# Projecting the next pair's q and k early in the odd steps, and laying both out in the same step

## The reference, cut to what matters

```python
mod = (_silu(c) @ wmod).reshape(16, 6, 1, -1)          # sa, ca, ga, sb, cb, gb
h = _layernorm(x) * (1 + ca) + sa
qkv = h @ W_qkv + b_qkv                                # 16 heads of 8 features
energy = jnp.einsum('bqhe,bkhe->bqhk', q, k)
attn = jax.nn.softmax(energy, axis=-1) / sqrt(E)
out = jnp.einsum('bihv,bvhd->bihd', attn, v).reshape(B, N, E) @ W_out + b_out
x = x + ga * out
h = _layernorm(x) * (1 + cb) + sb
x = x + gb * (quantise_fp6(h) @ quantise_fp6(weight).T + bias)   # blocks of 32
```

## Time and profile before

| | |
|---|---|
| median of 3 runs | 371.02 us (368.11 to 371.32) |
| profiled execution, its own time | 370.78 us |
| span of the profiled execution | 368.9 us |
| mean granted TensorE clock | 0.837 of full speed |
| PE busy | 304.0 us (82%) |
| VectorE, ScalarE, GpSimd busy | 245.1 (66%), 211.6 (57%), 174.5 us (47%) |
| DMA, mean busy share of 16 engines | 42.9% for the queue of SyncE |

### The profile page before, as it was taken

One profiled execution on the slowest core, in us unless ns is written; L12 is line 12 of the kernel. 1 busy time (PEld: TensorE's weight loads), 2 busy tenths in 40 slices (PEclk: granted clock), 3 DMA queues, 4 the chain that ended last, 5 costly groups with the idle time before them and its releaser, 6 DMA issues.

```text
span 368.9 us, 7149 instructions
## 1 busy us (share of the span) xinstructions
PE 304.0 (82%) x2506; PEld 175.0 (47%) x2506; DVE 245.1 (66%) x581; ACT 211.6 (57%) x404; POOL 174.5 (47%) x330
## 2 busy tenths in 40 slices
PE   1741997899969996999599987999699969999952
PEld 1211873455536453646255544546364636565521
DVE  5586895467957794579548784579557866984334
ACT  5470044478648862677357853677467745777720
POOL 5900133038563855265624765275535643547431
PEclk9966556599989995799759995799779996999985
DMA  5597079105930593128710692039602881010000
GB/s 151 170 306 156 26 245 227 50 1 228 202 92 32 230 206 73 44 114 237 157 30 16 240 225 57 30 124 253 131 30 96 248 177 33 18 46 4 17 14 14
DMA packets 23970, 43.81 MB, mean 119 GB/s; under 512 B 2144, under 2 KB 7408, under 8 KB 23936
## 3 DMA queue, kind: packets, MB, share of 16 engines
q1 hardware_dynamic: 23936, 43.37, 42.9%
HBM read 23.93 MB, written 18.91 MB: 116 GB/s over the span
## 4 chain that ended last, share of the span: by engine, by line
PE 37%; DMA 33%; POOL 12%; DVE 10%; issue 4%; SPq 2%; ACT 1%; POOLq 0%; DVEq 0%; ACTq 0%
DMA k_rows<-parts_dram 23%; PE ps_p L793 14%; DMA parts_dram<-qk_parts 10%; PE ps_o L823 9%; DVE neg_max L683 3%; POOL qk_parts L319 2%; POOL xh L296 2%; PE ps_pre L850 2%; POOL rstd L448 2%; PE ps_pre L834 2%; POOL xm L300 2%; POOL h L304 2%; PE ps_pre L844 2%; PE ps_post L881 2%; PE ps_o L867 1%
## 5 line engine op out<-in xcount | busy, mean ns | idle before, releaser
L683 DVE TENSOR_REDUCE neg_max<-ps_p 128x2 f32<-128x512 f32 x256 | 167.1, 684 | 84.7 <-PE ps_p L793 83.3
L552 ACT ACTIVATE probs<-ps_p 128x512 f32<-128x512 f32 x256 | 146.2, 594 | 93.1 <-PE ps_p L808 90.9
L793 PE MATMUL ps_p<-k_rows,q_rows 62*128 62x256 f32 x512 | 132.8, 364 | 35.3 <-DMA k_rows<-parts_dram 35.3
L793 PEld LDWEIGHTS ps_p<-k_rows,q_rows 62*128 62x128 f32 x512 | 87.2, 221 | 100.8 <-issue 48.2
L808 PE MATMUL ps_p<-q_rows,k_rows 64*128 64x256 f32 x512 | 130.1, 354 | 1.8 <-ACT probs L552 1.8
L823 PE MATMUL ps_o<-probs,v_aug 128*32 128x256 f32 x1024 | 90.5, 442 | 0.2 <-ACT probs L552 0.2
L808 PEld LDWEIGHTS ps_p<-q_rows,k_rows 64*128 64x128 f32 x512 | 84.0, 211 | 7.3 <-ACT probs L552 5.6
L429 POOL CAST max_parts<-neg_max 128x16 fp32r<-128x16 f32 x32 | 6.3, 197 | 88.8 <-DVE neg_max L683 88.8
L823 PEld LDWEIGHTS ps_o<-probs,v_aug 128*32 128x32 f32 x1024 | 23.5, 116 | 22.0 <-issue 7.6
L448 POOL TENSOR_TENSOR rstd<-ve,minus_half 128x2 f32<-128x2 f32 x16 | 11.3, 704 | 37.7 <-DVE ve L608 37.7
L319 POOL TENSOR_TENSOR qk_parts<-qk_full_sb,qk_parts 128x512 fp32r<-128x512 f32 x14 | 17.9, 1275 | 11.5 <-ACT qk_parts L533 11.5
(11 more groups left out here) (104 smaller groups left out, 362.0 us busy)
## 6 DMA issues: line engine op xcount, KB each, us to landing
parts_dram<-qk_parts SPq DMA_DIRECT2D x8, 1024.0 KB, 4.5
parts_dram<-qk_parts SPq DMA_DIRECT2D x16, 512.0 KB, 3.7
q_rows<-parts_dram SPq DMA_DIRECT2D x16, 512.0 KB, 6.9
k_rows<-parts_dram SPq DMA_DIRECT2D x16, 512.0 KB, 9.3
modb<-mod_rows_dram SPq DMA_DIRECT2D x16, 256.0 KB, 3.3
out_dram<-out_sb SPq DMA_DIRECT2D x16, 128.0 KB, 1.7
x_all<-in_L_attn_x_dram SPq DMA_DIRECT2D x1, 1536.0 KB, 9.3
q_rows<-maxT SPq DMA_DIRECT2D x64, 8.0 KB
```

Source lines behind the costliest of these rows:

```text
L552: act.activation(probs[:, v % 2, u % 4, :], ps_p2[:, u % 2, :], ACT.Exp).then_inc(exp_done, 1)
L683: dve.tensor_reduce(neg_max[:, half, :, r, j], ps_p1[:, (16 * b + s) % P1_BANKS, :].rearrange("p (q k) -> p q k", q=QT), AX_X, ALU.max, ne ...
L793: ins = pe.matmul(ps_p1[:, (16 * b + s) % P1_BANKS, t * T:(t + 1) * T], q_rows[64 * r:64 * r + ROWS1, slot, i, e, t * P:(t + 1) * P], k_ro ...
```

## The change

q is projected in slot 2 and k in slot 4 of the odd step, v of batch b+1 in slot 7 of every step. ACT saves hT in slot 1 behind the exponential, hdT in slot 2, q in slot 3, k in slot 5 ahead of onT, v in slot 7. GpSimd makes both low parts right behind `split_max(b+1, 0)`, ahead of `attn_weights(b)`. SyncE stores both parts ahead of `place_max(b+1, 0)` and issues the four layout loads in the same odd step, between `place_max(b+1, 0)` and `place_max(b+1, 1)`. Waits on `ps_pre` follow the new order: k waits for q's save, v for k's, half 0 of the maxima for v's.

```diff
@@ SyncE
             for b in range(-1, NB + 2):
-                early, late = low_pair(b), low_pair(b - 1)
+                p = low_pair(b)
...
-                if late is not None:
-                    lay_out(late, 0)
-                    lay_out(late, 1)
                 if has(b + 1) and b >= 0:
                     load_modb(b + 1)
                 if has(b - 2):
                     store(b - 2)
+                if p is not None:
+                    store_parts(p, 0)
+                    store_parts(p, 1)
                 if has(b + 1):
                     place_max(b + 1, 0)
-                if early is not None:
-                    store_parts(early, 0)
-                    store_parts(early, 1)
+                if p is not None:
+                    for kind in range(2):
+                        for r in range(2):
+                            lay_out(sp, p, kind, r)
                 if has(b + 1):
                     place_max(b + 1, 1)
@@ GpSimd
                     split_max(b + 1, 0)
+                if low_pair(b) is not None:
+                    low_part(pool, low_pair(b), 0, q_saved)
+                    low_part(pool, low_pair(b), 1, k_saved)
                 if has(b):
                     attn_weights(b)
                 if norm_pair(b) is not None:
                     normalise1(norm_pair(b), 0)
-                if low_pair(b) is not None:
-                    low_part(pool, low_pair(b), 0, q_saved)
...
-                if low_pair(b) is not None:
-                    low_part(pool, low_pair(b), 1, k_saved)
@@ ScalarE
-                    if s == 0 and pre is not None:
+                    if s == 1 and pre is not None:
                         save_hT(pre)
...
-                    if s == 1 and has(b - 2):
+                    if s == 2 and has(b - 2):
                         save(b - 2, hdT_full, f_full, hdT[:, :], ps_post[:, 0:T], hdT_saved)
-                    if s == 4 and has(b + 1):
-                        save_v(b + 1)
+                    if s == 3 and pre is not None:
+                        save_qk(pre, 0, q_full, q_saved)
+                    if s == 5 and pre is not None:
+                        save_qk(pre, 1, k_full, k_saved, ps_post if pre < 2 else ps_pre)
                     if s == 5 and has(b - 1):
                         save(b - 1, onT_full, y_full, onT[:, :], ps_post[:, 0:T], onT_saved)
-                    if s == 5 and pre is not None:
-                        save_qk(pre, 0, q_full, q_saved)
+                    if s == 7 and has(b + 1):
+                        save_v(b + 1)
...
-                    if s == 10 and pre is not None:
-                        save_qk(pre, 1, k_full, k_saved, ps_post if pre < 2 else ps_pre)
@@ TensorE
+                    if s == 2 and pre is not None:
+                        project_qk(pre, 0, q_full, ps_pre)
...
-                    if s == 4 and has(b + 1):
-                        project_v(b + 1)
+                    if s == 4 and pre is not None:
+                        if pre < 2:
+                            project_qk(pre, 1, k_full, ps_post, (modT_ready, 1), (k_saved, 2 * pre))
+                        else:
+                            project_qk(pre, 1, k_full, ps_pre, (q_saved, 2 * (pre + 1)))
...
-                    if s == 5 and pre is not None:
-                        project_qk(pre, 0, q_full, ps_pre, (v_saved, b + 2))
...
+                    if s == 7 and has(b + 1):
+                        project_v(b + 1, (k_saved, 2 * (pre + 1) if pre is not None else 0))
                     if s == 8 and has(b + 1):
-                        transpose_max(b + 1, 0, (q_saved, 2 * (pre + 1) if pre is not None else 0), (v_saved, b + 2))
-                    if s == 10 and pre is not None:
...
+                        transpose_max(b + 1, 0, (v_saved, b + 2))
```

More of the change, by code:

```diff
@@ L320, in low_part, with lay_out @@
                               qk_parts[:, p % 2, kind, 0, :].bitcast(F32), ALU.subtract).then_inc(low_ready, 1)
+        def lay_out(eng, p, kind, r):
+            wait(eng, (parts_stored[kind], 16 * (1 + kind) * (p + 1)), (p2_full, 16 * 2 * (p - RING + 1)))
+            if p < RING:
+                eng.wait_ge(rows_filled[p], 2)
+            rows = q_rows if kind == 0 else k_rows
+            by_row = parts_dram[p, kind].rearrange("(i r d) q t -> r (d q) i t", r=2, d=D)
+            dst = rows[64 * r:64 * r + QUAD, p % RING, :, :, :].rearrange("a i e t -> a i (e t)")
+            eng.dma_start(dst.bitcast(F32), by_row[r]).then_inc(laid_out[p % RING], 16)
         block = ctx.enter_context(nc.Block())
@@ L354, in store_parts @@
                                      ).then_inc(parts_stored[1], 16)
[L356 to L365, removed]
             def place_max(b, half):
@@ L388, in _ @@
             store_parts(0, 1)
-            lay_out(0, 0)
-            lay_out(0, 1)
+            for kind in range(2):
+                for r in range(2):
+                    lay_out(sp, 0, kind, r)
             sp.wait_ge(rows_ready, 1)
@@ L835, in transpose_x, with project_v @@
                 ins.then_inc(xT_full, 1)
-            def project_v(b):
-                wait(pe, (hT_saved, 2 * (b // 2 + 1)), (maxT_saved, 2 * b))
+            def project_v(b, *before):
+                wait(pe, (hT_saved, 2 * (b // 2 + 1)), (maxT_saved, 2 * b), *before)
                 if b == 0:
@@ L955, in _ @@
                     if s == 14 and has(b + 1):
-                        transpose_max(b + 1, 1, (k_saved, 2 * (pre + 1) if pre is not None else 0),
-                                      (maxT_saved, 2 * b + 3))
+                        transpose_max(b + 1, 1, (maxT_saved, 2 * b + 3))
                     if s in (13, 15) and has(b):
```

## The result

The changed kernel takes **345.06 us** in the median of 4 runs (344.02 to 345.97), against 371.13 us for the kernel before (4 runs): ratio 0.931, 95% interval 0.926 to 0.937. The profiled execution took 344.02 us, its span is 342.2 us.

What follows compares the result with a forecast made beforehand. PE's waits for k's layout, paid as idle time and slow clock, were taken as the bound. Six pairs save 23.8 us, pair 1 adds 0.5, one slow pair 3: 20.3 off 370.78 gives 350.5 us, range 338 to 369.

Steps and rivals of the forecast that it cites:

- case A: Whole kernel: the sum of the terms holds, 350.5 us, range 344 to 357; chance 0.42.
- The timing inside the odd step: Odd step, from slot 0: k's low part done at 11.2 us, first load issued at 14.9, k's layout landed at 28.1.
- the step on what is late next: Slot 8': half 1 of the maxima, queued behind the loads, lands near 28.7 us; PE waits 0.7 us.
- Rival C: Slots 8' and 12': half 1 isn't held back, no waits, a pair takes 34.6 us, kernel 340 us; chance 0.15.
- The pair: Each of six pairs: 34.6 us plus a wait of 0.7 us makes 35.3, for 39.3 before.
- moving v costs nothing new: Projecting v in slot 7, not slot 4: same four matmuls, v needed only in the next step, no added cost.
- The sixth pair: Last of the six pairs, counted at 35.3 us like the others; the six together 211.8 us.
- The clock: Six pairs: waits of 0.8, 1.2 and 0.7 us leave it at 1.00, save one slow pair costing 3 us.
- Rival B: Slot 8': the wait is some 2 us, half clock follows, a pair takes 38.0 us, kernel 364 us; chance 0.25.
- Pair 1: First steps: slot 8 waits for the copy at 61.5 us, slot 12 at 65.5 to 66.5; counted as +0.5 us.
- Rival D: Slots 1 to 5: ACT saves pile up at half clock, 41.5 us a pair, kernel 385 us; chance 0.13.
- E: Whole kernel: nothing changes, as the copy of half 1 takes back exactly what the layout gives; chance 0.05.

Runs made afterwards that it cites:

- the loads alone: Kernel before with only the four layout loads moved to the odd step, behind the stores and ahead of half 1 of the maxima: 377.1 us, ratio 1.026.
- the copy in ACT's queue: Changed kernel with half 1 of the maxima issued by ScalarE's own queue in odd steps, behind its save in slot 14: 356.0 us, ratio 0.956.
- the kernel with half loads: Kernel before with half of the layout loads' data left out for pairs 1 to 7, as many transfers: 335.5 us, ratio 0.898.
- all three edits: Changed kernel with onT saved ahead of k, split_max(b+1, 1) before modulate2's last product, v and hdT in old slots where no pair is projected: 342.2 us, ratio 0.926.

## Why the prediction was right

The forecast was 350.5 us, rounded to 351, and 345 came, by the mechanism of case A, with some luck in the pair and the clock. By its steps:

- **The timing inside the odd step.** k's low part ends 11.5 us after slot 0 (forecast 11.2), the first load is issued at 15.6 (14.9), k's layout lands at 28.0 (28.1), the second scores of slot 8' start at 28.5 (half 1 at 28.7). The rows of before, laid end to end in the new order, gave these within 0.7 us.
- **The wait that follows.** It moved from slot 12' to slot 8', behind the loads in the queue, as the step on what is late next has it. Shown by the loads alone (39.3 us of waits for half 1 where 26.5 for the layout were) and by the copy in ACT's queue (no wait). Its size is 0 to 0.5 us a pair, 0.2 in the mean, against 0.7. Rival C is out. The Trainium skill (DMA: Bandwidth & Descriptors, "Queues, rings and completion order") has both sides, ring order within a queue and completion that need not follow it; here the copies were held up behind the loads of their queue, 7 times of 7 in the kernel with the loads alone.
- **The pair.** 35.2 us against 35.3, but that it came so near is luck: three waits were smaller than forecast, by 1.2 us in all, and two terms were missing, of 0.5 and some 0.8 us. onT's wait is 0.78 (forecast 1.2), q's 0.50 (0.8). Not in the sum was the wait of PE in slot 14 for `max_parts`, 0.5 to 0.7 us, twice a pair: the row for it stood in the late steps of before (0.68 us in one), and I took 15.0 us for a late step without asking what was in it, so the even half had it and the odd half not. And "moving v costs nothing new" was wrong by 0.4 us a step, together with hdT's save; the late steps show it. The slow clock of a pair before was worked out from a pair of 32.6 us, and the kernel with half loads has 33.3 at full clock.
- **The sixth pair** was mis-sized. I took 35.3 for all six, but the stretch from step 11 to step 13 takes 33.0 us (transposes of oT at 249.74 and 282.70). Its first half takes 17.5 us as in the others; its second takes 15.5, as a late step, for it ends in step 13, which has no transposes of x and no q of a next pair. The six take 209.0, not 211.8: 2.8 of the 6.5 us that were missing.
- **The clock.** "I take the clock to stay at 1.00, save for one pair" held without the exception: the pair after pair 1 took 35.2 at 1.00, another 3 us, for the half clock behind slot 8 of pair 1 was over by 67 us. The reason given was too bold, though. The rows had only waits of some 3.8 us, and I set waits of 0.7 to 1.2 against them as safe. The other kernels show the half clock behind waits of 0.89, 1.08, 1.13 and 1.31 us. The forecast 1.2 us for onT lies among these; that 0.78 came, and that the clock held, is in part luck. Rival B was nearer than its chance of 0.25 says: a like thing happens with loads 5 us later, at the wait of slot 12' in place of 8'. Its 364 us is no check of its sum, which has a wait of 1.1 us in it (the copy at 29.1, slot 8' at 28.0) where its condition says some 2; with 2 us it gives 38.9 us a pair and 369. The Trainium skill (TensorE: Matmul & The Clock Gate, "HAM oscillation — how this bites in real kernels") tells of a kernel whose clock was throttled behind each wait for a transfer. The runs agree for the waits of 1.08, 1.54, 1.63, 1.97 and 2.50 us named above, and disagree for those of 0.84 us and less, and for 1.30 and 1.76.
- **Pair 1.** Slot 8 waited until 61.87 (forecast 61.5); the transposes of oT in step 1 came at 73.7, 1.9 us sooner than before, where I had +0.5. Of that the tail gave back 1.8 (59.5 us from the last such transposes to the end, 57.7 before), whose steps are 0.4 longer each.

Rival D's build-up of saves on ACT is there only as the short waits for q's save and onT, and E's balance isn't.

Where did the 26.8 us between the profiled executions come from? 26.5 us of waits for the layout went; 2.6 us came for the maxima, and the short waits for onT, q's save, `max_parts` and hdT (5.1, 3.4, 7.7 and 1.8 us) grew from 2.4 to 18.0 us. The view of the earlier trace rows has for the kernel before, with none for q's save:

```profile
PE ps_pre L857 <- POOL max_parts L431: 1.4, 2, 0.7
...
PE ps_post L895 <- ACT hdT L556: 0.5, 1, 0.5
PE ps_post L881 <- ACT onT L556: 0.5, 1, 0.5
```

By the waits some 18 us are left over, and PE's busy time, 19.5 us shorter for the same matmuls, says where they are: in the slots at half clock that are gone (forecast 2.9 a pair, 17 in six). Half of the loads' data in the kernel before bears on it from the other side: 34 us or more gained where 26.5 of waits went, with the clock still at 0.91 in one pair.

What stays open is which waits the clock bears. Their length alone doesn't decide. It stayed at 1.00 behind all named waits in slot 8' of 0.84 us and less, and fell behind those of 1.08, 1.31, 1.54, 1.63, 1.97 and 2.50 us, for 3 to 10 us. But it also stayed behind waits of 1.03, 1.30 and 1.76 us (all three edits) and of 1.33 us (pair 1 of the changed kernel, run again). Equal waits went either way within one run: of 1.13 us for `max_parts` (kernel before with half loads), and of 0.86 to 0.90 us for the exponential (copies in ACT's queue). No run tells what else decides.

## What to carry to other kernels

When a transfer is issued earlier, look for the small one that it overtakes: it now lands behind the large one, and if its reader comes sooner the wait only changes its name. A wait of PE has two prices, the idle time and the slow slots behind it, and the second need not shrink with the first: loads issued 5 us later (20.4 after slot 0 in place of 15.6) cost 19 us between the medians, with 11 us of waits in the profile. Once the long wait is gone, the order of single instructions on the other engines is worth 5 us in each of two cases, but such gains stop where the next landing stands.

## What the runs showed of the hardware

- Two copies of 8 KB issued behind four loads of 512 KB in one queue held PE for 5.6 us in the mean (loads alone), and in pair 1 of the changed kernel for 1.97 us. With the same copies in another engine's queue that wait was gone, though the transfer engines were 97% busy.
- Issuing these two copies took 1.3 us of ScalarE's queue and kept PE waiting for 0.9 us a pair; the kernel was 2 to 3% slower.
- A wait of PE of 1.63 us was followed by some 10 us at a granted clock of 0.50, one of 2.50 us by some 3 us of it, beginning 1 us after the wait had ended, one of 1.76 us by none. In one run five equal waits of 1.13 us were followed by the half clock twice. The length of the wait alone doesn't tell what it costs.
- Between the kernel before and the changed one, 19.5 of 26.7 us of span are PE's busy time: the same 2506 matmuls at a higher mean clock.
